# Splitting the mixture's weights against a PSUM copy, and loading its rows in finer parts

## The reference, cut to what matters

```python
x = x + _L0_attn_ref(_layernorm(x), ...)      # 8 x 512 tokens of 128 channels
x = x + _L0_ffn_ref(_layernorm(x), ...)       # the mixture that the change is in
x = x + _L1_attn_ref(_layernorm(x), ...)
x = x + _L1_ffn_ref(_layernorm(x), ...)

def _L0_ffn_ref(x, rw1, rb1, rw2, rb2, ew1, eb1, ew2, eb2):
    B, T, C, E, K, CAP, H = (8, 256, 128, 8, 2, 512, 512)
    ...
    logits = jax.nn.relu(x @ rw1 + rb1) @ rw2 + rb2
    vals, ids = jax.lax.top_k(logits, K)
    probs = jax.nn.softmax(vals, axis=-1)
    ...
    disp = jnp.zeros((E, CAP, Cx), x.dtype).at[ids_f, pos_c].add(xr * keep[:, None])
    h = jax.nn.relu(jnp.einsum('enc,ech->enh', disp, ew1) + eb1[:, None, :])
    eo = jnp.einsum('enh,ehc->enc', h, ew2) + eb2[:, None, :]
    y = eo[ids_f, pos_c] * (probs_f * keep)[:, None]
    return y.reshape(Bx, Tx, K, Cx).sum(axis=2)
```

## Time and profile before

| | |
|---|---|
| median of 3 runs | 928.3 us (927.37 to 928.76) |
| the profiled execution | 927.65 us |
| its span, first to last instruction | 925.6 us |
| mean granted TensorE clock | 0.962 of full speed |
| busy: PE, DVE, ACT, POOL | 774.7, 693.2, 622.2, 632.3 us |
| L635, scatters of rows, x64 | 65.5 us busy, 1.02 us each |
| L652, scatters of outputs, x32 | 34.3 us busy, 1.07 us each |

### The profile page before, as it was taken

How to read it: one execution, slowest core, us unless ns; L and a number is a source line. 1 busy time by engine, 2 the same in 40 slices (tenths; PEclk the granted TensorE clock), 3 DMA queues, 4 the chain that set the end, 5 groups by cost and what they waited for, 6 DMA issues and landing times.

```text
span 925.6 us, 18384 instructions
## 1 busy us (share of the span) xinstructions
PE 774.7 (84%) x6154; PEld 469.3 (51%) x6154; DVE 693.2 (75%) x2078; ACT 622.2 (67%) x932; POOL 632.3 (68%) x414
## 2 busy tenths in 40 slices
PE   4965765669998689468787989999999999999997
PEld 1343221224543357323233756767776777777775
DVE  7769899985777558498999878776666666666664
ACT  3755233323455367248778988888888888989895
POOL 4008899730577727558798997686868686868695
PEclk9987899899999899879999999999999999999999
DMA  5999300008200030252600000000000000000000
GB/s 150 118 120 202 115 0 0 18 3 211 69 21 7 3 101 26 68 149 58 204 1 1 1 1 2 13 1 11 0 11 0 8 4 0 11 0 11 0 13 13
DMA packets 52761, 40.47 MB, mean 44 GB/s; under 512 B 6028, under 2 KB 44703, under 8 KB 52703
## 3 DMA queue, kind: packets, MB, share of 16 engines
q1 hardware_dynamic: 49630, 37.28, 18.5%
q0 software_dynamic: 3072, 2.51, 0.9%
HBM read 18.07 MB, written 14.88 MB: 36 GB/s over the span
## 4 chain that ended last, share of the span: by engine, by line
POOL 24%; PE 18%; issue 14%; DVE 14%; ACT 6%; DMA 1%; POOLq 0%; DVEq 0%; ACTq 0%; SPq 0%
POOL scratch L725 20%; PE PS L1874 17%; DVE scratch L1635 2%; DVE resid L1537 2%; DVE stats L1375 1%; DVE scratch L1643 1%; POOL disp L635 1%; POOL resid L711 1%; PE PS L1881 1%; ACT scratch L1163 1%; ACT scratch L1159 1%; DVE resid L1388 1%; DVE A L1400 1%; DVE scratch L1378 1%; ACT A L1094 1%
## 5 line engine op out<-in xcount | busy, mean ns | idle before, releaser
L725 POOL TENSOR_TENSOR scratch<-scratch 128x1024 f16<-128x1024 f32 x128 | 273.0, 2135 | 84.5 <-ACT scratch L1163 82.3
L1822 DVE SCALAR_TENSOR_TENSOR resid<-PS,coef,resid 128x128 f32<-128x128 f32 x512 | 144.0, 344 | 108.8 <-PE PS L1874 103.4
L1874 PEld LDWEIGHTS PS<-A,scratch 128*128 128x128 f16 x3456 | 203.4, 98 | 37.9 <-POOL scratch L725 4.9
L1874 PE MATMUL PS<-A,scratch 128*128 128x128 f16 x3456 | 217.1, 219 | 3.9 <-POOL scratch L725 1.6
L1874 PE MATMUL PS<-A 128*128 (+1 forms) x768 | 186.8, 379 | 0.8 <-DVE A L1666 0.2
L1159 ACT ACTIVATE scratch<-PS,cols 128x512 f32<-128x512 f32 x256 | 163.9, 683 | 25.9 <-PE PS L1874 19.0
L1163 ACT ACTIVATE scratch<-scratch 128x1024 f16<-128x1024 f32 x128 | 135.3, 1057 | 5.0
L1874 PE MATMUL PS<-scratch,ident 128*128 128x512 f32 x160 | 89.4, 681 | 51.9 <-DVE scratch L1341 51.9
L594 POOL TENSOR_TENSOR scratch<-A 128x1024 f32<-128x1024 f32 x32 | 76.0, 2384 | 73.2 <-DVE A L1310 56.2
L1874 PEld LDWEIGHTS PS<-A 128*128 128x128 f16 x768 | 70.7, 98 | 66.6 <-issue 0.7
L635 POOL DMA_INDIRECT disp<-A,scratch x64 | 65.5, 1023 | 36.4 <-issue 30.0
(11 more groups left out here) (334 smaller groups left out, 1321.0 us busy)
## 6 DMA issues: line engine op xcount, KB each, us to landing
A<-A SPq DMA_DIRECT2D x22, 256.0 KB, 7.5
y_rows<-zeros SPq DMA_DIRECT2D x8, 512.0 KB, 6.0
A<-y_rows SPq DMA_DIRECT2D x16, 256.0 KB, 3.5
disp<-zeros SPq DMA_DIRECT2D x4, 528.0 KB, 21.6
A<-disp SPq DMA_DIRECT2D x4, 528.0 KB, 6.0
resid<-in_L_attn_x SPq DMA_DIRECT2D x8, 256.0 KB, 4.0
A<-scratch SPq DMA_DIRECT2D x8, 256.0 KB, 6.9
A<-in_L_ffn_ew SPq DMA_DIRECT2D x1, 2048.0 KB, 12.4
```

Of the source, the lines that this page charges most:

```text
L725: pool.tensor_tensor(h_low[n % 4], h_full[n % 2], h_high[n % 4], SUB).then_inc(S("m1_low"), 1)
L1822: last = STT(out=resid[:, g, :], in0=bank(4 + e % 2)[:, t * C:(t + 1) * C], scalar=coef[b % 2][:, t, e:e + 1], in1=resid[:, g, :], op0=MUL ...
L1874: return nc.tensor.matmul(o, l, r, start=start, stop=stop)
```

## The change

The functions `high_made`, `beside_made` and `high_at` are new. (1) Behind the high part of the first six k, ACT also copies that high part from SBUF to two PSUM banks (`weights0_beside`: banks 0 and 1 for even k, 2 and 3 for odd), and VectorE's low part reads it there. From k = 2 on, a copy waits for the low part of k - 2, whose banks it takes. (2) The first three high parts run in the batch loop, at the end of its iterations 5, 6 and 7. (3) `eb2_rep` is copied behind the six low parts instead of ahead of them. (4) `disp` is loaded in parts of 1, 1, 3 and 3 experts. (5) Batch 0 of `y_rows` is loaded in two halves on the semaphores `s_disp[0]` and `[1]`, and `combine(0)` adds the first two tiles before it waits for the second half; the loads of batch 2 wait for nothing. (6) The unread passes are 30 ahead of the barrier and 6 behind it, in bank 4 instead of bank 3.

```diff
--- before.py
+++ after.py
@@ -381,7 +381,20 @@
         e0_hl1 = A2[:, :].bitcast(f16).rearrange("p (e s n) -> p e s n", e=E0, s=2)
         e0_hl2 = A3[:, :].bitcast(f16).rearrange("p (e s n) -> p e s n", e=E0, s=2)
         E0_SPLITS = 2
+        EARLY, BESIDE = 3, 6
+
+        def high_made(k):
+            return at(E0_SPLITS + (k if k < EARLY else 2 * k if k < BESIDE else k + BESIDE))
+
+        def beside_made(k):
+            return at(E0_SPLITS + (EARLY + k if k < EARLY else 2 * k + 1))
+
+        def high_at(k):
+            return bank(k % 2 * 2, 2)
+
         PARTS = ((0, 0), (0, 1), (1, 0))
+        XD_PARTS = ((0, 1), (1, 2), (2, 5), (5, E0))
+        XD_PART_OF = (0, 1, 2, 2, 2, 3, 3, 3)
 
         r7 = carve(7)[:, 688:688 + 2 * TILES].rearrange("p (s n) -> p s n", s=2)
         nm7 = carve(7)[:, 752:752 + TILES]
@@ -494,15 +507,22 @@
             sp.wait_ge(s_scattered[1], 16 * TOP0 * NT * (B - 5))
             sp.wait_ge(s_scattered[2], 16 * TOP0 * NT)
             dv = disp.rearrange("(n p) c -> p n c", p=128)
-            for k in range(E0 // 2):
-                sp.dma_start(xd[:, bts(k, 2 * NT), :], dv[:, bts(k, 2 * NT), :]).then_inc(s_disp[k], 16)
+            for k, (low, high) in enumerate(XD_PARTS):
+                part = slice(low * NT, high * NT)
+                sp.dma_start(xd[:, part, :], dv[:, part, :]).then_inc(s_disp[k], 16)
 
             sp.wait_ge(s_eo, 16 * E0 * NT)
             sp.wait_ge(S("split_low"), at(E0_SPLITS + 7))
             yv = y_rows.rearrange("(k n p) c -> k p n c", k=TOP0, p=128)
             for b in range(B):
-                if b >= 2:
-                    sp.wait_ge(s_fetched[b % 2], X_LOADS + 16 * TOP0 * (b // 2))
+                if b == 0:
+                    for half in range(2):
+                        for k in range(TOP0):
+                            part = slice(half * NT // 2, (half + 1) * NT // 2)
+                            sp.dma_start(fetched[k][:, part, :], yv[k][:, part, :]).then_inc(s_disp[half], 16)
+                    continue
+                if b >= 3:
+                    sp.wait_ge(s_fetched[b % 2], X_LOADS + 16 * TOP0 * ((b - 1) // 2))
                 for k in range(TOP0):
                     sp.dma_start(fetched[k][:, bts(b, NT), :], yv[k][:, bts(b, NT), :]).then_inc(s_fetched[b % 2], 16)
 
@@ -868,6 +888,18 @@
             deviation_x5(0)
             deviation_o(1)
             xT5_copy(0)
+            def weights0_high(k):
+                hl, w = ((e0_hl1, e0w1), (e0_hl2, e0w2.rearrange("p e i c -> p e (i c)")))[k // 4]
+                two = slice(2 * (k % 4), 2 * (k % 4) + 2)
+                A_(hl[:, two, 0, :], w[:, two, :], ACT.Copy, scale=SCALE).then_inc(S("split_high"), 1)
+
+            def weights0_beside(k):
+                hl = (e0_hl1, e0_hl2)[k // 4]
+                if k >= 2:
+                    act.wait_ge(S("split_low"), at(E0_SPLITS + k - 2))
+                act.wait_ge(S("split_high"), high_made(k))
+                A_(high_at(k), hl[:, 2 * (k % 4):2 * (k % 4) + 2, 0, :], ACT.Copy).then_inc(S("split_high"), 1)
+
             for b in range(B):
                 for h in range(HC0):
                     relu5(b, h)
@@ -884,18 +916,18 @@
                     square_o(2)
                 elif b + 2 < B:
                     deviation_o(b + 2)
-            def weights0_high(k):
-                hl, w = ((e0_hl1, e0w1), (e0_hl2, e0w2.rearrange("p e i c -> p e (i c)")))[k // 4]
-                two = slice(2 * (k % 4), 2 * (k % 4) + 2)
-                A_(hl[:, two, 0, :], w[:, two, :], ACT.Copy, scale=SCALE).then_inc(S("split_high"), 1)
-
+                if b >= B - EARLY:
+                    act.wait_ge(s_wm, 32)
+                    act.wait_ge(s_scattered[0], 16 * TOP0 * NT * 4)
+                    weights0_high(b - B + EARLY)
+            for k in range(EARLY):
+                weights0_beside(k)
             act.wait_ge(S("lg_less"), at(0))
             A_(tmpb[:, :], tmpa[:, :], ACT.Exp).then_inc(S("lg_exp"), 1)
-            act.wait_ge(s_wm, 32)
-            act.wait_ge(s_scattered[0], 16 * TOP0 * NT * 4)
             act.wait_ge(s_scattered[1], 16 * TOP0 * NT * (B - 5))
-            for k in range(6):
+            for k in range(EARLY, BESIDE):
                 weights0_high(k)
+                weights0_beside(k)
             stage_end(act, 5)
 
 
@@ -1462,19 +1494,18 @@
                 if b + 2 < B:
                     add_o(b + 2)
             TT(tmpa[:, :], top0[:, 1, :], top0[:, 0, :], SUB).then_inc(S("lg_less"), 1)
-            dve.wait_ge(s_eb2_mm, 1)
-            st.done(V.tensor_copy(eb2_rep, bank(6, 2).rearrange("p k (e c) -> p (k e) c", c=C)))
-
             def weights0_low(k):
                 hl, w = ((e0_hl1, e0w1), (e0_hl2, e0w2.rearrange("p e i c -> p e (i c)")))[k // 4]
                 two = slice(2 * (k % 4), 2 * (k % 4) + 2)
-                dve.wait_ge(S("split_high"), at(E0_SPLITS + k))
-                STT(out=hl[:, two, 1, :], in0=w[:, two, :], scalar=SCALE, in1=hl[:, two, 0, :],
+                dve.wait_ge(S("split_high"), beside_made(k) if k < BESIDE else high_made(k))
+                STT(out=hl[:, two, 1, :], in0=w[:, two, :], scalar=SCALE, in1=high_at(k) if k < BESIDE else hl[:, two, 0, :],
                     op0=MUL, op1=SUB).then_inc(S("split_low"), 1)
 
             TT(pick2, pickg[:, 0], pickg[:, 1], ADD)
-            for k in range(6):
+            for k in range(BESIDE):
                 weights0_low(k)
+            dve.wait_ge(s_eb2_mm, 1)
+            st.done(V.tensor_copy(eb2_rep, bank(6, 2).rearrange("p k (e c) -> p (k e) c", c=C)))
             dve.wait_ge(S("lg_exp"), at(0))
             st.done(TS(tmpa[:, :], tmpb[:, :], 1.0, None, ADD))
             st.done(V.reciprocal(tmpa[:, :], tmpa[:, :]))
@@ -1530,14 +1561,18 @@
 
 
             def combine(b):
-                dve.wait_ge(s_fetched[b % 2], X_LOADS + 16 * TOP0 * (b // 2 + 1))
-                for k in range(TOP0):
-                    for t in range(NT):
-                        g = b * NT + t
-                        last = STT(out=resid[:, g, :], in0=fetched[k][:, g, :], scalar=coef0[:, k, g:g + 1],
-                                   in1=resid[:, g, :], op0=MUL, op1=ADD)
-                    if k < TOP0 - 1:
-                        links.done(last)
+                if b:
+                    dve.wait_ge(s_fetched[b % 2], X_LOADS + 16 * TOP0 * ((b + 1) // 2))
+                for part in ((0, 1), (2, 3)) if b == 0 else (range(NT),):
+                    if b == 0:
+                        dve.wait_ge(s_disp[part[0] // 2], BACK[part[0] // 2] + 16 + 16 * TOP0)
+                    for k in range(TOP0):
+                        for t in part:
+                            g = b * NT + t
+                            last = STT(out=resid[:, g, :], in0=fetched[k][:, g, :], scalar=coef0[:, k, g:g + 1],
+                                       in1=resid[:, g, :], op0=MUL, op1=ADD)
+                        if k < TOP0 - 1:
+                            links.done(last)
                 last.then_inc(S("moe_added"), 1)
                 dve.wait_ge(S("moe_added"), at(b))
                 token_stats(b).then_inc(S("x_var"), 1)
@@ -1590,7 +1625,7 @@
                 dve.wait_ge(S("gate_high"), at(m))
                 TT(gate_hl[:, 1, c], whole_gate(m), gate_hl[:, 0, c], SUB).then_inc(S("gate_low"), 1)
 
-            dve.wait_ge(S("split_high"), at(E0_SPLITS + 8))
+            dve.wait_ge(S("split_high"), high_made(8))
             for low, w, high in ((u1_hl[:, 1, :], u_1[:, :], u1_hl[:, 0, :]), (u2_hl[1], u_2[:, :, :], u2_hl[0]),
                                  (ur_hl[:, 1, :], u_r[:, :], ur_hl[:, 0, :])):
                 STT(out=low, in0=w, scalar=SCALE, in1=high, op0=MUL, op1=SUB)
@@ -2067,13 +2102,13 @@
             for e in range(E0):
                 last = mm(tile(bank(6 + e // 4), e % 4), spread[:, e, :], eb2[:, :])
             last.then_inc(s_eb2_mm, 1)
-            unread(3, 20)
+            unread(4, 30)
             stage_end(pe, 5)
-            unread(3, 18)
+            unread(4, 6)
 
 
             def transpose_rows(e):
-                pe.wait_ge(s_disp[e // 2], BACK[e // 2] + 16)
+                pe.wait_ge(s_disp[XD_PART_OF[e]], BACK[XD_PART_OF[e]] + 16)
                 pe.wait_ge(S("xdT"), at(e, 2))
                 transposes(bank(e % 2), xd[:, bts(e, NT), 0:C]).then_inc(S("trd"), 1)
```

## The result

| | before | after |
|---|---|---|
| median of 6 runs each, us | 927.84 (927.00 to 928.91) | 923.80 (922.25 to 925.18) |
| ratio of the medians, 95% interval | | 0.9956 (0.9946 to 0.9966) |
| profiled execution, us | 927.65 | 923.42 |
| its span, us | 925.6 | 921.2 |

The change makes the kernel faster by 4.0 us (927.84 - 923.80), against 4.0 in the forecast. The chain by engine of the changed kernel's page has hardly moved from the earlier trace rows: a local change does not show in shares.

What follows compares the result with a forecast made beforehand. No engine bounds the whole span; the chain over five engines does, at the hand-overs ending stages 5 and 6. Gains 2.4 + 0.85 + 0.77 = 4.0 us, from the median 928.3, give 924.3 us; range 923.2 to 926.8.

Steps and rivals of the forecast that it cites:

- One operand in PSUM: End of stage 5: VectorE's splits with one PSUM operand no longer stretch three GpSimd scatters; 2.4 us, bounds 1.5 to 2.5.
- the second rival: End of stage 5: VectorE's splits still hold GpSimd's scatters up, the 2.4 us go, 926.7 us; chance 0.09.
- Rows in finer parts: First load of scattered rows after stage 5: one expert instead of two lands sooner; 0.85 us, bounds 0 and 0.9.
- First rows back by halves: End of stage 6: first addition waits for two loads of 128 KB, not 256; 0.77 us, bounds 0.3 and 0.87.
- It is there: End of stage 6: second half lands 0.87 us after the first, within the 1.2 us of the first half's additions.
- The sum: Gains at the ends of stages 5 and 6: 2.4 + 0.85 + 0.77 = 4.0 us, all kept to the end.
- The barrier: End of stage 5: VectorE arrives at 323.7, 0.7 us later; TensorE's passes end at 325.0, rows come about 326.1; costs nothing.
- Unread passes: End of stage 5: 30 TensorE passes ahead of the barrier and six behind, instead of 20 and 18; worth zero.
- Clock: After stage 5's barrier: TensorE's idle gaps are too short for a fall, first experts' matmuls run at 2.4 GHz as before.
- The rival's 1.0 us: Clock low when the scattered rows arrive: VectorE's last low part of expert 0 some 1.0 us later, 925.3 us; chance 0.15.
- Expert 1's part: After stage 5: its load lands where the old first load did, wanted only 1.8 us after expert 0's; no wait.
- The pair as the bound: Stage 5's end: alternating ACT copies and VectorE splits decide from about 2.7 us a split; 929.8 us at 3; chance 0.05, including unseen loss.

Runs made afterwards that it cites:

- the quarters: The changed kernel with the first batch's rows loaded as eight loads of 64 KB and added tile by tile: 950.91 us, ratio 0.9944, on the third chip.

## Why the prediction was right

The time (924.3 forecast, 923.8 measured) and the three mechanisms hold, but each of the three terms came out above its upper bound, and one step that was priced at nothing carries the gain. Step by step:

- *One operand in PSUM*, 2.4 us with bounds of 1.5 and 2.5: measured 2.54, just above the upper bound, which was rounded down from that sum. The share I held back for VectorE's 0.10 us beside a scatter did not appear in the changed kernel; on the third chip two scatters near the first PSUM split take 1.03 and 1.09. The two kernels with SBUF operands show the mechanism; the second rival (GpSimd held up all the same) is out.
- *Rows in finer parts*, 0.85 us with bounds of 0 and 0.9: measured 1.09 against before and 1.14 with this part alone undone. The term was sized by the pace between loads (528 KB in 1.8 us), read where several were in flight together. By the issue-to-landing times, 264 KB less are worth 1.1 us, some 240 KB a us; why the first load is slower than that pace was not tested. The Trainium skill's page DMA: Bandwidth & Descriptors, section Anatomy of one DMA, gives its fixed 2 us and 436 GB/s for DMAs that GpSimd issues. These loads are SP's, so the 0.62 us that the prediction works out with it is no test of the page; measured here is 1.09. (Its two terms would make the sum 0.23 + 0.27 = 0.5 us smaller, not 0.4.)
- *First rows back by halves*, 0.87 - 0.10 = 0.77 us: measured 1.22 - 0.13 = 1.09, and 1.0 with this part alone undone. This term goes by the same pace and is too small by as much; the links were right. "It is there", of the second half, held in the changed kernel only by a little: in three of the experiments with halves VectorE waited 0.32, 0.39 and 0.55 us for it.
- *The sum*: 4.0 forecast, 4.7 measured in three places, of which the span kept 4.4. On the medians it is 4.0, within the spread of the runs; that the forecast is exact to half a microsecond is in part luck: the terms were 0.14, 0.24 and 0.32 too small, above the 4.3 of their bounds together, and what took the 0.7 off again (the offset of 0.29, and 0.4 between the span's gain and that of the medians) was in no term. The 0.5 us between 924.3 and 923.8 is the kernel before, whose median was 928.3 for the forecast and 927.84 in the result.
- *The barrier*: forecast 323.7, TensorE free at 325.0, rows at 326.1; the trace has 323.87, 325.3 and 326.1. The order of ACT and VectorE came out to 0.2 us, since every term of it had a row.
- *Unread passes*, "worth zero in the sum": right as a price and wrong as a description. Against the kernel before nothing was gained by them; but 20 and 18 passes would have cost 3.1 us in this place (that kernel is level with the one before). The sum should have had the line: passes behind the barrier, 18 × 0.22 = 4.0 us at the upper level and more at the lower (5.51 measured), against 2.4 us from the barrier at 323.7 to the rows at 326.1.
- *Clock*: it stayed at 1.00 as forecast. The rival's 1.0 us was in the right range: stage 6 grew by 0.34, 0.41 and 0.60 us in three kernels that had a low clock at its start (20 and 6 passes, high parts behind the loop, 30 and none), and by 1.5 in the one with SBUF operands, where the clock was low until 338 us, 7 us behind the first transposes. The argument for 1.00, a gap shorter than the 3.9 us, is weaker than it looked: with gaps of 2.11 and 2.45 us the clock still fell behind the first transposes in the kernel with three SBUF operands.
- *Expert 1's part, "no wait"*: TensorE waits 0.18 us for it, and the wait is hidden, as stage 6 has not grown.
- *The pair as the bound*: not by the 2.7 us a split that I named (a split takes 1.22). By the prediction's own terms a later barrier delays the transposes from (326.1 - 1.3 - 2.4 - 310.05) / 6 = 2.06 us a split on; 2.7 is about where the gain at the scatters is used up. Two edits of order bring a late barrier about: the high parts behind the loop (7.95 us of idle TensorE) and the bias copy ahead of the splits (5.64). Both of the change's moves, which the sum has at nothing, are needed for the gain.

## What to carry to other kernels

When a long VectorE instruction runs beside GpSimd work that is on the critical path, look at whether both of its inputs are in SBUF: moving one into PSUM cost ACT idle time here and gave GpSimd all of the stretch back. The price can be read from the rows: a scatter that starts beside such an instruction is stretched by nearly what is left of it. Before counting such a gain, walk every engine to the next barrier and list what stands on either side of it; here the scatters' 2.5 us were worth nothing until filler matmuls, the bias copy and three high parts had been moved. Where the first consumer needs a part of a load, split the first load alone, down to the size at which issue and further waits take more than the bytes give back (256 to 128 KB gained 1.1 us; 128 to 64 KB gained 0.26 at the first addition, and lost 0.1 to 0.8 by the last).

## What the runs showed of the hardware

- What two SBUF operands cost GpSimd depends on which scatters start beside them, and not on VectorE's busy time: six splits of 1.2 us back to back cost 2.54 us, the same six spread over 11 us cost 4.24. Each scatter that starts beside a split grows by 0.5 to 1.05 us; in the six splits that stand alone in the two experiments, by what was left of the split less 0.12 to 0.14 us. A scatter that was already running is not stretched, and VectorE does not slow at all.
- This goes on in stage 6 of the changed kernel, where two splits still read SBUF: the scatters that start beside them take 1.74 us, as in the earlier trace rows: stretched by 0.77, with 0.89 of the split left. They are off the chain there.

```profile
339.72 1.21 DVE L1501 SCALAR_TENSOR_TENSOR A<-A 128x1024 f16<-128x1024 f32 x1
340.04 1.74 POOL L672 DMA_INDIRECT y_rows<-A  x1 [0.30 <-DVE A L1535]
```

- Small loads: two of 128 KB land 2.1 to 2.3 us after their issue, where the pair of 256 KB took 3.5. SP spends 0.34 to 0.47 us on issuing one of 64 or 128 KB and 0.36 to 0.51 on one of 256 KB, but up to 1.6 us on one of the larger loads of `disp` (528 and 792 KB) behind others. So the "whatever its size" of the expectation for the quarters holds only up to 256 KB.
- The granted clock stayed at 1.00 over 2.0 us of idle time, six passes, and 0.8 us more; with 1.9 us in place of the 0.8 (rows in pairs) it stayed as well. Around this barrier it fell in or after every idle time of 3.9 us and more, but also behind shorter ones: 2.11 and 2.45 us with six passes between them, and in the kernel without GpSimd's waits 0.92, 1.03 and 1.73 us with four passes between them. The fall can come after the idle time: with no passes behind the barrier the clock was 1.00 through 4.21 us of it and the first transposes. A low start cost stage 6 0.3 to 0.6 us, and 1.5 where the clock stayed low for 6 us.
- One chip ran the kernels some 3% longer (957.34 against 927.65 us for the kernel before). In its four traces stage 5's last batch begins 18 to 25 us later and stage 6 takes 7 to 10 us more, with the mean granted clock of the kernel before at 0.948 against 0.957 and 0.959 on the other two. The cause of the gaps stays open.
